# Cross-attention in fp32 with high and low halves: the first q group woven into the weight folds, and projections with high and low inputs in one wide product

## The reference, cut to what matters

```python
def _lora_linear(x, W, A, B):
    return x @ W + SCALING * (x @ A @ B)          # SCALING 2.0, R 16
q = _lora_linear(hidden_states, Wq, Aq, Bq)       # 8 x 256 x 1024, 32 heads of 32
k = _lora_linear(traces, Wk, Ak, Bk)              # 8 x 256 x 256, 8 heads, each used by 4 q heads
v = _lora_linear(traces, Wv, Av, Bv)
scores = einsum('bhqd,bhtd->bhqt', q, k) / sqrt(32)
attn = softmax(scores)
context = einsum('bhqt,bhtd->bhqd', attn, v)
out = _lora_linear(context, Wo, Ao, Bo)
return hidden_states + out
```

## Time and profile before

| | |
|---|---|
| time, median of 3 runs | 694.38 us (693.0 to 696.91) |
| the profiled execution's own time | 695.28 us |
| its span | 693.5 us |
| PE, PEld busy | 98%, 84% |
| DVE, ACT, POOL busy | 66%, 68%, 53% |
| mean granted PE clock, as a share of full | 0.995 |

### The profile page before, as it was taken

One profiled execution on the slowest core, in us unless ns is written; L12 is line 12 of the kernel. 1 busy time (PEld: TensorE's weight loads), 2 busy tenths in 40 slices (PEclk: granted clock), 3 DMA queues, 4 the chain that ended last, 5 costly groups with the idle time before them and its releaser, 6 DMA issues.

```text
span 693.5 us, 16134 instructions
## 1 busy us (share of the span) xinstructions
PE 678.0 (98%) x5018; PEld 580.4 (84%) x5018; DVE 456.6 (66%) x886; ACT 474.5 (68%) x1470; POOL 366.5 (53%) x318
## 2 busy tenths in 40 slices
PE   8989999999999999999999999999999999999998
PEld 5878888888888888888888888888767788888886
DVE  4737787576566657656765765676767798855542
ACT  4638888888788878878887887888988443222220
POOL 3646733752673375357337535733976304866632
PEclk9989999999999999999999999999999999999999
DMA  9956674776577477657747765775877343655331
GB/s 272 338 152 197 190 206 134 193 204 177 152 184 205 131 199 192 178 149 191 200 129 197 193 180 145 196 206 148 213 185 239 125 156 133 230 183 178 126 110 73
DMA packets 103799, 124.70 MB, mean 180 GB/s; under 512 B 9280, under 2 KB 85312, under 8 KB 103760
## 3 DMA queue, kind: packets, MB, share of 16 engines
q1 hardware_dynamic: 103760, 124.23, 62.8%
HBM read 86.18 MB, written 38.01 MB: 179 GB/s over the span
## 4 chain that ended last, share of the span: by engine, by line
PE 91%; DMA 5%; SPq 2%; issue 1%; ACT 1%; DVE 1%; POOL 0%; DVEq 0%; POOLq 0%
PE banks L1391 37%; PE banks L1597 16%; PE banks L1409 10%; PE banks L1449 9%; PE banks L1436 8%; PE banks L1460 6%; DMA r_rows<-turned_sb 2%; PE banks L1427 2%; PE banks L1377 1%; PE banks L1378 1%; SPq L415 1%; DMA q_stack<-q_parts 1%; DMA scales<-bkv 1%; DMA q_parts<-q_stage 1%; DMA scales<-r_rows 1%
## 5 line engine op out<-in xcount | busy, mean ns | idle before, releaser
L1091 DVE TENSOR_REDUCE neg_max<-banks 128x2 f32<-128x512 f32 x256 | 176.6, 690 | 134.7 <-PE banks L1409 133.1
L890 ACT ACTIVATE banks<-banks,neg_max 128x256 f32<-128x256 f32 x512 | 231.0, 455 | 19.8 <-DVE neg_max L1091 19.7
L774 POOL TENSOR_TENSOR q_stack<-turned_sb,head_mask 8x512 fp32r<-8x512 f32 x128 | 137.3, 1073 | 201.9 <-DVE turned_sb L1117 196.9
L901 ACT ACTIVATE probs_t<-banks 128x512 f32<-128x512 f32 x256 | 154.6, 604 | 72.2 <-PE banks L1436 70.5
L1391 PE MATMUL banks<-x_lo,w_hi 128*128 128x256 f32 x512 | 145.3, 284 | 0.0
L1391 PE MATMUL banks<-x_hi,w_hi 128*128 128x256 f32 x512 | 145.1, 283 | 0.1
L1391 PE MATMUL banks<-x_hi,w_lo 128*128 128x256 f32 x512 | 145.1, 283 | 0.0
L1409 PE MATMUL banks<-k_stack,q_stack 96*128 96x256 f32 x512 | 110.6, 298 | 5.8 <-DMA q_stack<-q_parts 4.2
L890 ACT ACTIVATION_READ_ACCUMULATOR banks<-banks,neg_max 128x1 f32 x512 | 108.6, 212 | 0.0
L1409 PEld LDWEIGHTS banks<-k_stack,q_stack 96*128 96x128 f32 x512 | 80.0, 192 | 33.3 <-ACT banks L890 19.8
L1436 PE MATMUL banks<-q_stack,k_stack 104*128 104x512 f32 x256 | 107.8, 421 | 0.0
(11 more groups left out here) (168 smaller groups left out, 1311.1 us busy)
## 6 DMA issues: line engine op xcount, KB each, us to landing
q_stack<-q_parts SPq DMA_DIRECT2D x192, 128.0 KB, 3.8
q_parts<-q_stage SPq DMA_DIRECT2D x64, 256.0 KB, 2.6
raw<-ct SPq DMA_DIRECT2D x32, 256.0 KB, 4.8
raw<-xt SPq DMA_DIRECT2D x32, 256.0 KB, 4.3
scales<-r_rows SPq DMA_DIRECT2D x64, 128.0 KB
context<-ctx_stage SPq DMA_DIRECT2D x64, 128.0 KB, 2.1
stage<-xn SPq DMA_DIRECT2D x16, 512.0 KB, 5.0
w_hi<-context SPq DMA_DIRECT2D x14, 512.0 KB, 6.8
```

The source lines that it names most:

```text
L774: nc.gpsimd.tensor_tensor(q_stack[rows, u % RING, heads], turned_sb[rows, u % 2].unsqueeze(1).broadcast_to([M_ROWS, 2, S]), head_mask[rows ...
L890: last = nc.scalar.activation(score_bank[c % 2][:, S * h:S * (h + 1)], score_bank[c % 2][:, S * h:S * (h + 1)], ACT.Exp, bias=neg_max[:, u ...
L901: nc.scalar.activation(probs_t[:, u % 2, t, 2 * hp:2 * hp + 2, :].rearrange("p a b -> p (a b)"), st_bank[j % 2], ACT.Exp, scale=-1.0).then ...
L1091: nc.vector.tensor_reduce(out=neg_max[:, u % 2, 2 * c:2 * c + 2], in_=score_bank[c % 2].rearrange("p (h t) -> p h t", h=2), axis=AXIS, op= ...
```

## The change

Two edits. First, the prologue: the first q group is now group 2 and its steps stand behind folds 12 to 16, by a table `WEAVE` (for each Wq fold, which group gets how many steps; "n" are the next q groups); v comes after it in number, and gets its 24 steps in two parts. Of folds 8 to 15 PE adds 9, 11, 13 and 15, of the rest 16 and 20. The context loads of the next batch on SP's queue go one by one behind the stores of q groups, where four stood ahead of the first. ACT, DVE and SP take their lists in the new order, and the low half of q group 3 is taken in slot 1 in place of 0. Second, from slot 3 on, a group's high x high and high x low products are one matmul of 512 columns: the still operand is the high half, the moving one both halves, which now lie in one tile (`x_both`, `c_both`, `wkv_both`), and the result fills the bank, main part in its first 256 columns, high x low in the other 256. Low x high stays a matmul of 256 columns, added to the main part. DVE adds the second part in an instruction of its own, behind a semaphore `proj_part`. The prologue and the ramp keep three narrow steps (`narrow_step`, `narrow_low`).

```diff
-PROLOGUE = [("k", 0, 0), ("k", 1, 0), ("v", 0, 0), ("q", 0, 0), ("q", 1, 0), ("q", 2, 0),
+PROLOGUE = [("k", 0, 0), ("k", 1, 0), ("q", 0, 0), ("v", 0, 0), ("q", 1, 0), ("q", 2, 0),
             ("q", 3, 0), ("v", 1, 0)]
-PRO_Q = 3
+PRO_V = 3
+PRO_Q = (2, 4, 5, 6)
...
+WEAVE = (((),) + ((("v", 3),),) * 3 + ((("q", 3),),) * 3 + ((("q", 6),),)
+         + ((("q", 9),), (("v", 9),), (("v", 6), ("n", 3)), (("n", 9),), (("n", 9),), (("n", 9),), (("n", 9),), (("n", 9),)))
...
-        wkv_hl = [sb("wkv_hi", [P, KT, 2 * KV], F32R), sb("wkv_lo", [P, KT, 2 * KV], F32R)]
-
-        x_hl = [sb("x_hi", [P, KT, S], F32R), sb("x_lo", [P, KT, S], F32R)]
-        c_hl = [sb("c_hi", [P, KT, S], F32R), sb("c_lo", [P, KT, S], F32R)]
+        wkv_both = sb("wkv_both", [P, 2, KT, 2 * KV], F32R)
+
+        x_both = sb("x_both", [P, 2, KT, S], F32R)
+        c_both = sb("c_both", [P, 2, KT, S], F32R)
+        wkv_hl, x_hl, c_hl = ([t[:, i] for i in range(2)] for t in (wkv_both, x_both, c_both))
...
-            return f < FOLD_Q or f % 4 == 0 and f < FOLD_O
+            return f < FOLD_Q or f in (FOLD_Q + 1, FOLD_Q + 3, FOLD_Q + 5, FOLD_Q + 7, FOLD_Q + 8, FOLD_Q + 12)
...
-            load_context(1, 0, 1, 2, 3)
             stack_k(0, 1, 0)
             for g in range(4):
-                send_q(g, g + PRO_Q + 1)
+                send_q(g, PRO_Q[g] + 1)
+                load_context(1, g)
...
-            for j in range(4):
+            for j in range(3):
                 high(x_hl, j, x_hi_done, 2)
             proj_high("k", 1, 1, 1, None)
-            w_highs(*range(8))
-            w_highs(8, 9, 10)
+            high(x_hl, 3, x_hi_done, 2)
+            w_highs(*range(9))
             early_q_high(0)
-            w_highs(11, 12, 13)
+            w_highs(9, 10, 11, 12, 13)
...
+            def proj_low(kind, i, bank, group_id, splits, moves):
+                main, minor = (proj_bank[bank][:, S * n:S * (n + 1)] for n in range(2))
+                if kind == "v":
+                    dve.wait_ge(proj_mm, group_id + 1)
+                    need(dve, v_moved, moves)
+                    nc.vector.tensor_copy(v_new[:, i, :], main).then_inc(proj_part, 1)
+                    dve.wait_ge(proj_part, group_id + 1)
+                    nc.vector.tensor_tensor(v_new[:, i, :], minor, v_new[:, i, :], ALU.add).then_inc(proj_out, 1)
+                elif kind == "k":
+                    hi, lo = (k_stage[:, i, n, :] for n in range(2))
+                    dve.wait_ge(proj_hi, splits)
+                    nc.vector.scalar_tensor_tensor(out=lo, in0=main, scalar=-SCORE_SCALE, in1=hi,
+                                                   op0=ALU.mult, op1=ALU.subtract).then_inc(proj_part, 1)
+                    dve.wait_ge(proj_part, group_id + 1)
+                    nc.vector.scalar_tensor_tensor(out=lo, in0=minor, scalar=-SCORE_SCALE, in1=lo,
+                                                   op0=ALU.mult, op1=ALU.add).then_inc(proj_out, 1)
+                else:
+                    hi, lo = (q_stage[:, i % 2, n, :] for n in range(2))
+                    dve.wait_ge(proj_hi, splits)
+                    nc.vector.tensor_tensor(lo, main, hi, ALU.subtract).then_inc(proj_part, 1)
+                    dve.wait_ge(proj_part, group_id + 1)
+                    nc.vector.tensor_tensor(lo, minor, lo, ALU.add).then_inc(proj_out, 1)
...
-            proj_low("k", 0, 0, 0, 1, None)
-            for j in range(4):
+            narrow_low("k", 0, 0, 0, 1, None)
+            def x_low(j):
                 input_low(x_hl, j, x_hi_done, x_ready, j + 1)
-            proj_low("k", 1, 1, 1, 2, None)
-            w_pairs(*range(FOLD_Q, FOLD_Q + KT, 2))
-            proj_low("v", 0, 0, PRO_Q - 1, None, 0)
-            w_pairs(FOLD_Q + 8, FOLD_Q + 10)
+
+            x_low(0)
+            x_low(1)
+            narrow_low("k", 1, 1, 1, 2, None)
+            w_total(FOLD_Q)
+            w_total(FOLD_Q + 2)
+            x_low(2)
+            w_low(FOLD_Q + 1)
+            w_total(FOLD_Q + 4)
+            x_low(3)
+            w_low(FOLD_Q + 3)
+            w_total(FOLD_Q + 6)
+            w_low(FOLD_Q + 5)
+            w_low(FOLD_Q + 7)
+            w_low(FOLD_Q + 8)
             early_q_low(0)
+            w_total(FOLD_Q + 9)
+            w_pairs(FOLD_Q + 10)
+            narrow_low("v", 0, PRO_V % 2, PRO_V, None, 0)
             w_pairs(FOLD_Q + 12)
             early_q_low(1)
             w_pairs(FOLD_Q + 14)
...
-                if first and s == 0:
-                    proj_low("q", 3, EARLY % 2, EARLY, 6, None)
+                if first and s == 1:
+                    narrow_low("q", 3, EARLY % 2, EARLY, 6, None)
                 if s < FIRST:
                     return
                 if s == FIRST:
-                    proj_low("v", 1, 1, b * PER + (PRO - 1), None, b)
+                    (narrow_low if first else proj_low)("v", 1, 1, b * PER + (PRO - 1), None, b)
...
-            def group_step(kind, i, bank, k):
+            def narrow_step(kind, i, bank, k):
 
                 kt, product = divmod(k, 3)
                 w_part, t_part = ((0, 0), (0, 1), (1, 0))[product]
                 if kind == "q":
-                    lhs, rhs = w_hl[w_part][:, kt, P * i:P * (i + 1)], x_hl[t_part][:, kt, :]
+                    still, moving = w_hl[w_part][:, kt, P * i:P * (i + 1)], x_hl[t_part][:, kt, :]
                 elif kind == "k":
-                    lhs, rhs = wkv_hl[w_part][:, kt, P * i:P * (i + 1)], c_hl[t_part][:, kt, :]
+                    still, moving = wkv_hl[w_part][:, kt, P * i:P * (i + 1)], c_hl[t_part][:, kt, :]
                 else:
-                    lhs, rhs = c_hl[t_part][:, kt, P * i:P * (i + 1)], wkv_hl[w_part][:, kt, KV:2 * KV]
-                mm = nc.tensor.matmul(proj_bank[bank][:, 0:S], lhs, rhs, start=(k == 0),
-                                      stop=(k == GROUP_MM - 1))
+                    still, moving = c_hl[t_part][:, kt, P * i:P * (i + 1)], wkv_hl[w_part][:, kt, KV:2 * KV]
+                mm = nc.tensor.matmul(proj_bank[bank][:, 0:S], still, moving, start=(k == 0), stop=(k == GROUP_MM - 1))
+                if k == GROUP_MM - 1:
...
+            def group_step(kind, i, bank, k):
+
+                kt, piece = divmod(k, 3)
+                narrow, wide = (0, 2) if kt == KT - 1 else (2, 0)
+                if piece not in (narrow, wide):
+                    return
+                part = int(piece == narrow)
+                if kind == "q":
+                    still, moving = w_hl[part][:, kt, P * i:P * (i + 1)], x_both
+                elif kind == "k":
+                    still, moving = wkv_hl[part][:, kt, P * i:P * (i + 1)], c_both
+                else:
+                    still, moving = c_hl[part][:, kt, P * i:P * (i + 1)], wkv_both
+                cols = slice(KV, 2 * KV) if kind == "v" else slice(0, S)
+                if piece == narrow:
+                    mm = nc.tensor.matmul(proj_bank[bank][:, 0:S], still, moving[:, 0, kt, cols], start=False, stop=False)
+                else:
+                    mm = nc.tensor.matmul(proj_bank[bank].rearrange("p (a n) -> p a n", a=2), still, moving[:, :, kt, cols],
+                                          start=(k == 0), stop=(k == GROUP_MM - 1))
                 if k == GROUP_MM - 1:
                     mm.then_inc(proj_mm, 1)
...
-            for kt in range(KT):
-                if kt == 4:
+            starts = {"q": PRO_Q[0] * GROUP_MM, "v": PRO_V * GROUP_MM, "n": PRO_Q[1] * GROUP_MM}
+            for n, pieces in enumerate(WEAVE):
+                if n == 4:
                     pe.wait_ge(stack_lo_pool, 4)
-                fold_mms(FOLD_Q + kt)
-                for n in range(3):
-                    early_step(2 * GROUP_MM + 3 * kt + n)
-            for kt in range(KT):
-                fold_mms(FOLD_Q + KT + kt)
-                for n in range(9):
-                    early_step(3 * GROUP_MM + 9 * kt + n)
+                fold_mms(FOLD_Q + n)
+                for group, steps in pieces:
+                    for _ in range(steps):
+                        early_step(starts[group])
+                        starts[group] += 1
...
-                    group_step(kind, i, j % 2, step)
+                    (narrow_step if s < FIRST else group_step)(kind, i, j % 2, step)
```

13 lines of the change are left out of this document (8 added, 5 removed).

## The result

The changed kernel takes 695.45 us (median of 20 runs, 692.65 to 698.27), the kernel before 692.82 on the same chip (20 runs, 690.63 to 696.91): ratio 1.0034, 95% interval 1.0020 to 1.0048. It is slower by 0.34%, which is under the 0.5% that the prediction counts as no change, and outside its range of 679 to 688.5 in any case.

What follows compares the result with a forecast made beforehand. The prediction took PE as the bound, without idle time from 127 to 480 us. Its terms, 8.2 - 1.5 + 5.1 - 0.5 = 11.3 us, took 695.28 to 684.0, less 0.9 gives 683.0; range 679 to 688.5.

Steps and rivals of the forecast that it cites:

- the two large terms, 2.5 and 2.9: Prologue and ramp: first scores 2.5 us sooner, and 2.9 us lost at the low clock behind them won back.
- 0.9 us above the median: Whole kernel: runs' median 694.38 us against 695.28 profiled, so 0.9 us was subtracted from the forecast of 684.0.
- the 0.9 us of wait at slot 2: Old ramp: PE's wait of 0.95 us for exponentials goes, counted as 0.9 us gained.
- The 1.2 us of wait foreseen at scores 4: Ramp: the second q group's copies land after PE is ready for these scores, 1.2 us lost.
- 8.2 in all: Steady groups, batches 0 to 6: 0.0122 us saved per matmul that goes, 84 x 8 of them, 8.2 us.
- Rival (a): Steady groups: a wide matmul costs 0.234 to 0.239 us and saves little; 690 to 691.5 us, chance 10%.
- its two reasons: Wide matmul at 0.234 to 0.239 us: only the streaming counts, or the two runs are fetched as two.
- 1.5 us in all: Slots 17 to 20: second k subtractions delay exponentials, PE waits 0.3 us in each of 7 batches, less idle time.
- 0.5 us lost: Last batch: v and q subtractions 0.46 us later hold up PE's folds; 0.5 us lost, bounds 0 and 2.
- 5% for slower: Whole kernel: DVE becomes the bound through second subtractions ahead of row maxima; 698 to 720 us, chance 5%.

Runs made afterwards that it cites:

- before again: The kernel before the change, unchanged, run and profiled once more; 692.54 us, ratio to itself 0.9999.
- after again: The whole change, unchanged, run and profiled once more on the chip of the kernels beside it; 694.71 us, ratio 1.0029 to the kernel before.
- weave only: The first edit alone on the kernel before: woven prologue, narrow products and one subtraction per group everywhere; 693.81 us, ratio 1.0011.
- wide only: The second edit alone on the kernel before: old prologue, wide products from slot 3 on; 693.21 us, ratio 0.9997.
- part wide: The whole change with old prologue, k groups and last batch narrow, wide products grouped within a slot; 688.75 us, ratio 0.9935 to the kernel before.

## Why the prediction was wrong

**The prologue: the step that failed.** "They land at 43. That is before PE gets there: the first scores start at 44.3, 2.5 us sooner. With no wait of 2.8 us ahead of it the clock should not fall: at 0.71 for 10 us, 2.9 us were lost". The new side of this was nearly right (45.0 to 45.5 in seven profiles with the weave, 46.2 in one). The old side was one execution in which copies were late, PE waited 2.64 us, and the clock fell within this wait. The same prologue has its first scores at 43.87, 43.92, 44.07, 44.27 and 44.51 in five other profiles, at full clock. So the two large terms, 2.5 and 2.9, were no property of the kernel. I had even noted that the profile lay 0.9 us above the median and subtracted that from the sum in place of asking which stretch it came from. What is left: PE adds two more folds, and reaches the first scores 1.25 us later than in before again; the 0.9 us of wait at slot 2 go, as foreseen, where they were there. At slot 3 after again is 0.18 us behind; the five profiles of the old prologue lie at 53.4 to 54.1 us there, the eight with the weave at 53.5 to 54.7. The 1.2 us of wait foreseen at scores 4 were 0 to 0.74.

**Batch 0: no term for it.** From slot 3 to 35 after takes 62.73 and 62.74 us, weave only 62.12, wide only 62.49, before again 61.75; part wide takes 60.59, and 61.77 with the weave. (The first profile of before has 59.72, after its late start.) I had walked the DMA queue only as far as the second q group. Two waits of after there go back to transfers, DVE's for the Wo LoRA factors and PE's for the first normalized context, whose scales come back late:

```profile
59.25 0.29 DVE L1049 CAST lora_o<-stage 128x256 fp32r<-128x256 f32 x1 [2.01 <-DMA stage<-b4o]
...
71.71 1.07 PE L1513 MATMUL banks<-probs_t,v_sb 128*32 128x256 f32 x16 [0.92 <-DVE ctx_stage L1151]
```

DVE's wait for the factors is 1.25 to 2.83 us in all eight profiles with the weave and 0 to 0.91 us in the six with the old prologue, so it is longer with the weave. That the context loads now stand between the stores is a reason for late transfers that I can argue and did not test. Waits for a normalized context are in before again too (0.54 us at 77.31), and the one profile of wide only has 62.49 as well, so not all of the loss needs the weave.

**Steady groups: mechanism right, size off.** Said: 0.346 us a kt, 0.0122 for each matmul that goes, 8.2 in all. Measured: 0.351; without slot 20 a batch is 0.49 us shorter, 0.0051 for each of 96, some 3.4 us in seven batches. The pair of wide and narrow alone saves 0.007; a part comes back beside it, where the step from one score to the second goes from 0.140 to 0.146 us and from there to the transposed ones from 0.119 to 0.121 (means without the outer tenths). The price of a wide matmul came from a stretch in which there is no other width. The trace of before had a nearer row, transposed scores of 512 columns among narrow steps:

```profile
403.19 0.40 PE L1436 MATMUL banks<-q_stack,k_stack 104*128 104x512 f32 x1
403.42 0.28 PE L1391 MATMUL banks<-x_hi,w_hi 128*128 128x256 f32 x1
```

Over 101 of them between 130 and 470 us the mean step, without the outer tenths, is 0.2335. Rival (a) had the price of 0.234 right; of its two reasons, the two runs are ruled out, and that only columns count does not fit either, since the pair then costs as much as three narrow ones.

**DVE: the term in the right slot, by the wrong chain.** I had found 0.8 us to spare between maxima, exponentials and scores, and taken 0.3 us a batch less DVE's idle time, 1.5 us in all. The chain that counts there goes over DVE's copy, POOL's placing and the transposed scores, and had nothing to spare: in before again POOL starts at 388.05 and PE at 389.54, 1.49 us later; in after 390.48 and 391.95, 1.47 later. The chain goes back at least to ACT's high half of the first k group, for which DVE waits 0.45 us in after. Slot 20 is 0.47 us longer in each of the batches 2 to 6, as much as one second subtraction takes, but the two are not the same: with both k groups narrow 0.33 of it goes and 0.14 stays, and that goes too only where the wide products are also grouped within the slot (part wide). What holds the 0.14 no run shows. By the order of DVE's rows the 0.33 are the first k group's; the second's stands behind the copy. With both k groups narrow a batch is 0.27 shorter, since 16 matmuls more are issued.

**The last batch.** Said: 0.5 us lost. PE waits for second subtractions as foreseen:

```profile
491.78 0.50 PE L1421 MATMUL banks<-lora_o 128*128 128x512 f32 x1 [0.69 <-DVE q_stage L1113]
```

Slots 4 and 8 are 0.45 us longer each (in part wide slot 8 is not, but slot 4 still is: PE waits there for the last v group of batch 6, which is wide), but from slot 223 to the first product wide only takes 102.13 us, before again 102.15, after again 103.30 and weave only 100.97: the waits are hidden by others, and the spread is larger than the term.

**The sum as measured**, after again against before again: 1.25 at the first scores, -1.07 in the ramp, 0.99 in batch 0, -0.15 in the batches 1 to 6, 1.15 in the last: 2.2 us, as 692.3 and 690.2 say. How much of batch 0 and of the last batch is the change's and how much the draw's stays open, and with it what makes up the 0.3% by which the kernel is slower: one or two profiles of each kernel can't tell, and the timed ratios of weave only and wide only, 0.0011 and -0.0003, add up to less than the 0.0029 of both within their intervals.

**The chances.** 5% for slower was far too little, and it all stood on DVE as the bound. A rival that said "the wait at the first scores is this execution's" was missing; it would have left 8.2 - 1.5 - 0.5 = 6.2 us and no more. Even that would have been called faster; the price of a wide matmul and slot 20 take 4.8 and 1.3 of it (3.4 against 8.2, and 6 x 0.47 = 2.8 against 1.5) and leave 0.1.

## What to carry to other kernels

Before a wait in a single profile becomes a term of the sum, look for what makes it differ between executions: a wait for DMA and a dip of the clock behind it are the first to doubt, above all when that profile lies above the median. Take the price of a matmul from a row with the same neighbours, not only of the same width. When an operation is added to an engine, follow every instruction behind it to its reader, by way of POOL too; the chain with the least to spare is not always the one with the obvious consumer. A change that saves little per instruction pays only where its own extra work is off the chain: left out of the k groups and of the last batch, with the wide ones grouped within a slot and the old prologue, it is worth 0.65%.
